# Transposing a stored matrix inside the last layer of one graph network instead of ahead of the next one

## What is computed

```python
h = jnp.maximum(_layernorm(x), 0.0); x = x + _L0_gnn_ref(h, edge_index, ...)   # sum over edges, two dense layers
h = jnp.maximum(_layernorm(x), 0.0); x = x + _L1_gnn_ref(h, edge_index, ...)   # two normed sums over edges
h = jnp.maximum(_layernorm(x), 0.0); x = x + _L2_gnn_ref(h, edge_index, ...)   # four layers, each:
#   z = segment_sum(h[src], dst) + h;  z = relu(z @ W1[i] + b1[i]) @ W2[i] + b2[i];  h = relu(batchnorm(z))
h = jnp.maximum(_layernorm(x), 0.0); x = x + _L3_gnn_ref(h, edge_index, ...)   # mixhop:
#   xj = segment_sum(val[:, None] * xj[col], row)      (the edges in the other direction)
```

## Time and profile before

| | |
|---|---|
| time, median of 3 runs | 1275.44 us (1271.63 to 1276.02) |
| the profiled execution: its own time | 1276.86 us |
| its span, first to last instruction | 1275.3 us |
| PE busy | 1142.3 us, 90% of the span |
| DVE, ACT busy | 687.3 us (54%), 456.4 us (36%) |
| mean granted clock of PE | 0.969 |

### The profile page before, as it was taken

How to read it: one execution, slowest core, us unless ns; L and a number is a source line. 1 busy time by engine, 2 the same in 40 slices (tenths; PEclk the granted TensorE clock), 3 DMA queues, 4 the chain that set the end, 5 groups by cost and what they waited for, 6 DMA issues and landing times.

```text
span 1275.3 us, 19427 instructions
## 1 busy us (share of the span) xinstructions
PE 1142.3 (90%) x6308; PEld 660.3 (52%) x6308; DVE 687.3 (54%) x2175; ACT 456.4 (36%) x1348; POOL 8.5 (1%) x31
## 2 busy tenths in 40 slices
PE   1677899998989999998998998993899998999997
PEld 1556667665554555545445445452544554444644
DVE  8999999995452235455364453466343334533211
ACT  1558988886571122211202113116211213631100
POOL 1000000000000000000000000000000000000000
PEclk9999999999999999999998998996999998999999
DMA  3100000001001000134132231338996313410001
GB/s 63 31 2 2 1 2 10 1 2 47 6 11 25 15 9 1 38 81 89 32 80 55 51 83 33 79 69 150 254 261 170 83 43 82 106 49 22 13 25 29
DMA packets 208801, 70.31 MB, mean 55 GB/s; under 512 B 180999, under 2 KB 208074, under 8 KB 208699
## 3 DMA queue, kind: packets, MB, share of 16 engines
q1 hardware_dynamic: 121131, 43.37, 14.7%
q10 hardware_dynamic: 87568, 25.67, 9.3%
HBM read 20.71 MB, written 28.26 MB: 38 GB/s over the span
## 4 chain that ended last, share of the span: by engine, by line
PE 73%; DVE 11%; ACT 4%; SPq 4%; DMA 3%; issue 3%; DVEq 1%; ACTq 0%; POOL 0%; POOLq 0%
PE PS L1156 48%; PE PS L886 7%; DVE HPb L750 4%; SPq L2077 4%; PE PS L2422 2%; PE PS L1453 2%; PE PS L875 2%; PE PS L851 2%; PE PS L1909 2%; PE PS L1915 2%; DMA ADJ<-adj_d 2%; DVE HPb L701 2%; ACT HPb L2399 1%; DMA deg_d<-ADJ 1%; PE PS L1945 1%
## 5 line engine op out<-in xcount | busy, mean ns | idle before, releaser
L1156 PE MATMUL PS<-ADJ,HPb 125*128 125x500 bf16 (+2 forms) x2450 | 492.7, 357 | 11.6 <-DMA ADJ<-adj_d 4.5
L1156 PEld LDWEIGHTS PS<-ADJ,HPb 125*128 125x128 f16 x2450 | 240.7, 99 | 258.0 <-issue 41.1
L922 ACT CAST ADJ<-PS 126x72 f32 (+7 forms) x784 | 193.4, 316 | 52.0 <-PE PS L886 18.4
L1156 PE MATMUL PS<-ADJ,Zf 125*128 125x500 bf16 (+2 forms) x1050 | 202.1, 352 | 0.0
L886 PE MATMUL PS<-HPb 128*128 128x150 bf16 (+3 forms) x784 | 191.8, 346 | 3.4 <-ACT ADJ L922 2.7
L1156 PEld LDWEIGHTS PS<-ADJ,Zf 125*128 125x128 f16 x1050 | 102.4, 97 | 93.8 <-issue 1.3
L750 DVE TENSOR_SCALAR HPb<-XRf,Zf 128x176 bf16<-128x176 f16 (+2 forms) x588 | 135.8, 291 | 1.3 <-PE PS L886 0.3
L875 PEld LDWEIGHTS PS<-HPb 128*128 128x128 bf16 x642 | 85.6, 141 | 61.7 <-issue 37.1
L1700 DVE CUSTOM_DVE_ANT_0 HPb<-ADJ,HPb 125x625 bf16<-125x625 bf16 x125 | 101.2, 810 | 3.7
L875 PE MATMUL PS<-HPb 128*128 128x25 bf16 x642 | 91.4, 214 | 13.0 <-DVE HPb L750 12.6
L1808 DVE TENSOR_SCALAR Zf<-PS,B_L 128x500 f32<-128x500 f32 (+2 forms) x28 | 19.1, 683 | 141.7 <-PE PS L1915 141.7
(11 more groups left out here) (325 smaller groups left out, 1024.3 us busy)
## 6 DMA issues: line engine op xcount, KB each, us to landing
adj_d<-ADJ ACTq DMA_DIRECT2D x25, 700.0 KB
HPb<-y_d SPq DMA_DIRECT2D x19, 187.5 KB, 2.5
HPb<-di_d SPq DMA_DIRECT2D x10, 250.0 KB, 3.5
adj_d<-ADJ ACTq DMA_DIRECT2D x25, 81.2 KB
ADJ<-in_x SPq DMA_DIRECT2D x1, 1562.5 KB
q_d<-HPb SPq DMA_DIRECT2D x25, 62.5 KB
HPb<-di_d SPq DMA_DIRECT2D x5, 305.2 KB
HPb<-s_d ACTq DMA_DIRECT2D x5, 250.0 KB, 6.7
```

The costliest lines, as they stand in the source:

```text
L922: e.copy(to, WPS[group % BANKS][0:PD, t0 * RESTS[q]:t1 * RESTS[q]] .rearrange("p (t d) -> p t d", t=t1 - t0)).then_inc(s_mv, 1)
L1156: mm = e.matmul(accs[q], H[0:PN, t, q, 0:P], cols, start=(t == 0 and (two or q == 0)), stop=(t == NT - 1 and (two or q == 1)), skip_group_ ...
```

## The change

Three things change. The stores of `keep` start one network earlier: seven of them (one a chunk) in phase `L1b`, behind ACT's copy of the sum, and six in each of the first three layers of `L2`; the last layer has none. `ADJT` is laid 240 elements (`T0`) further up, so that its first five pieces only cover columns that the chunks up to the same number have left. And `turned(0)` to `turned(4)` are issued by SP inside the last layer, each once its chunk is summed; `turned(5)` waits for the last sum, and `turned(6)` stands behind the load of the weights, ahead of the six row loads. `rows_out` now stands between `turned(3)` and `turned(4)`.

```diff
+        T0 = -(-(NT - 1) * (AW - NP) // 16) * 16
+        ADJT = ADJ[:, :, :].rearrange("p t d -> p (t d)")[:, T0:T0 + NT * NP].rearrange("p (t s) -> p t s", t=NT)
+        assert all(TURNED[c][1] + T0 <= sum(SPANS[c]) * PN for c in range(NC - 2))
...
             if act:
+                e.wait_ge(s_adj, 3)
+                e.dma_start(adj_d[N:NP], columns(0, 0, NP - N)).then_inc(s_kept, 16)
                 e.wait_ge(s_inv, 2)
...
                     e.activation(first_of(LOS, c), sums(NC + c, c)[1], ACT.Copy, scale=INVL).then_inc(E1b["lo"], 1)
+                    keep(c)
                     e.wait_ge(s_stat, n)
...
-                e.wait_ge(s_dout, 102)
-                rows_out(s1_d, DEG)
+                e.wait_ge(s_kept, 16 * (2 * NT + 1))
+                for c in range(NC - 2):
+                    if c == NC - 3:
+                        e.wait_ge(s_dout, 102)
+                        rows_out(s1_d, DEG)
+                    done(E2["agg"], (LAYERS - 1) * NC + c + 1)
+                    turned(c)
...
-                        if c < NC - 1:
-                            keep(l * (NC - 1) + c)
-                        if (l, c) == (0, 2):
-                            keep(NT - 1)
+                        if c < NC - 1 and not last:
+                            keep(NC + l * (NC - 1) + c)
...
                 e.wait_ge(s_dout, 118)
-                e.wait_ge(s_kept, 16 * (2 * NT + 1))
                 done(E2["agg"], NC * LAYERS)
-                turned(0)
-                turned(1)
+                turned(NC - 2)
                 done(E2["d2"], NC * LAYERS)
                 e.dma_start(WB[:, 0:2 * P].rearrange("p (q n) -> p q n", q=2),
                             a["L3_gnn_l1_w"][0:2].rearrange("q p n -> p q n")).then_inc(s_wt, 16)
+                turned(NC - 1)
                 e.wait_ge(s_bn["tr"], LAYERS * NB)
                 for c in range(NC - 1):
                     row_in(beside(c), di_d, c, SPANS3)
-                for c in range(2, NC):
-                    turned(c)
```

More of the change, by code:

```diff
@@ L120, in build @@
     KEPT = PN // 16 * 16
-    assert NT * NP <= NT * AW and KEPT < PN and LAYERS * (NC - 1) + 1 == NT
+    assert NT * NP <= NT * AW and KEPT < PN and NC + (LAYERS - 1) * (NC - 1) == NT
     TURNED, s0 = [], 0
@@ L275, in build @@
         IOC = XRf[:, RW:RW + HC * P // 2].bitcast(F16).rearrange("p (n c) -> p n c", c=HC)
-        ADJT = ADJ[:, :, :].rearrange("p t d -> p (t d)")[:, 0:NT * NP].rearrange("p (t s) -> p t s", t=NT)
+        T0 = -(-(NT - 1) * (AW - NP) // 16) * 16
+        ADJT = ADJ[:, :, :].rearrange("p t d -> p (t d)")[:, T0:T0 + NT * NP].rearrange("p (t s) -> p t s", t=NT)
+        assert T0 + NT * NP <= NT * AW
+        assert all(TURNED[c][1] + T0 <= sum(SPANS[c]) * PN for c in range(NC - 2))
         adj_d = dram("adj_d", [NP, NT, P], BF16)
@@ L1559, in layers, with columns, keep @@
                     sum_tiles(E1, HP, c, (acc, acc), False, 1, before)
+            def columns(t, p0, p1):
+                v = ADJ[p0:p1, t, 0:P]
+                return bass.AP(v.tensor, v.offset, [v.ap[0], [PN, NT], [1, P]])
+            def keep(t):
+                for p0, p1 in ((0, KEPT), (KEPT, PN)):
+                    e.dma_start(adj_d[t * PN + p0:t * PN + p1], columns(t, p0, p1)).then_inc(s_kept, 16)
             if dve:
@@ L1647, in row_piece, with turned @@
                     e.dma_start(ROWP[0:PN], bcast(v[r * PIECE:(r + 1) * PIECE], PN)).then_inc(s_dout, 16)
+                def turned(c):
+                    if c >= 2:
+                        e.wait_ge(s_turned[c % 2], c // 2 * 16)
+                    s0, s1 = TURNED[c]
+                    e.dma_start(ADJT[:, :, s0:s1], adj_d[s0:s1].rearrange("s t d -> s (t d)"), transpose=True)\
+                     .then_inc(s_turned[c % 2], 16)
                 done(E0["d2"], NC)
@@ L1786, in close_row_sums @@
                 e.sem_inc(s_dout, 1)
[L1788 to L1795, removed]
             def layer2(l, last):
@@ L1840, in layer2 @@
                 if act:
-                    if l == 0:
-                        e.wait_ge(s_adj, 3)
-                        e.dma_start(adj_d[N:NP], columns(0, 0, NP - N)).then_inc(s_kept, 16)
                     for c in range(NC):
```

## The result

The changed kernel takes 1280.56 us in the median of 20 runs (1278.13 to 1284.7), the kernel before 1275.85 in 20 runs beside it. The ratio is 1.0037 with a 95% interval of 1.0022 to 1.0052: 2.8 to 6.6 us slower. I had forecast 1273.0, with 1266 to 1281 as the range, so the sign is wrong, though the time lies just inside the range. The profiled execution took 1283.77 us, with a span of 1282.1.

What follows compares the result with a forecast made beforehand. PE's waits and slow stretches in L3a were taken to lose 9.9 us. A new stall of 5.5 plus a slow stretch of 1.9 less 9.9 gave -2.5 us: from a median of 1275.44 to 1273.0, range 1266.0 to 1281.0.

Steps and rivals of the forecast that it cites:

- What bounds it, and what could be gained: PE in L3a from `hidden1(0)` at 902.00 us: two waits and their slow stretches lose 9.9 us, the most to be gained.
- The first stall: PE at 907.90 us, 2.32 us behind ACT, plus 1.7 at half clock; blamed on transposes beside the load of `s1_d`.
- The stores: Stores in L1b make the last chunk's square root 0.9 us late, under 2.6 us of cover: cost 0.
- Transposes 0 to 3: SP under the last layer: 40.0 us from 809.99, ending near 850.5, all hidden with 8 us spare.
- the landing of the row loads: Six row loads behind three transposes on SP land at 907.0 us; `hidden1(0)` at 907.5 against 902.00, +5.5 us.
- "`turned(4)`: ... I take 3 us": SP's queue: 12.1 us for 496 rows plus 3 for `rows_out` ahead (bounds 0 and 7), ending 873.9.
- The rival "order within the queue": `turned(4)` data wait for the last packet of `rows_out`, up to 7 us: +1.5, 1276.9 us; chance 0.15.
- Its sign in the profile: SP's queue: `turned(4)` held 18 us or more would show the queue's order at work.
- The slow stretch: PE behind the new stall ahead of `hidden1(0)`: 1.9 us lost, as after the wait at 959.24.
- The weights: Issued by SP behind `turned(5)`, landing at 890.5 us against 890.15 wanted; costs nothing, hidden behind the input block's 2.64 us wait.

Runs made afterwards that it cites:

- tenth: Changed kernel, `rows_out` issued by ACT, `turned(4)` at once, no wait for `rows_out` landing, row loads then load of `s1_d` ahead of `turned(6)`: 1265.59 us.
- eleventh: Changed kernel with `turned(5)` and `turned(6)` behind the row loads and held until ACT's first load of `s1_d` has landed: 1265.78 us.
- first experiment: Changed kernel with the six row loads issued ahead of `turned(6)`: 1274.15 us, ratio to before 0.997.
- second experiment: Changed kernel with the six row loads issued ahead of both `turned(5)` and `turned(6)`: 1272.38 us, ratio to before 0.9962.
- 6: Changed kernel with `rows_out` issued by ACT, `turned(4)` not waiting for closed row sums, row loads ahead of `turned(6)`: 1269.86 us.
- seventh experiment: Changed kernel with `rows_out` in 125 pieces of 100 bytes instead of 3125 of 4, so its output differs: 1270.14 us.
- third: Changed kernel with `rows_out` issued by ACT in place of SP: 1276.57 us, ratio to before 0.9995.
- fifth: Changed kernel with `rows_out` issued by ACT and no SP wait for the closed row sums ahead of `turned(4)`: 1273.74 us.
- eighth: Changed kernel, `rows_out` issued by ACT, `turned(4)` at once, `turned(5)` waiting for closed row sums but not the landing of `rows_out`: 1270.28 us.
- fourth experiment: Kernel before with only the stores of `keep` moved as in the change: 1274.08 us, ratio to before 0.9977.

## Why the prediction was wrong

**What bounds it, and what could be gained: right.** I had counted 9.9 us of loss behind 902.00. Against 77.0 us in the tenth and eleventh, the kernel before has 10.8 us more, and 8.0 in its second profile. The 10.8 is 0.9 more than my bound; 0.49 us of it is a wait of PE for a transpose at 927.87 that I had left out. The first stall was indeed the transposes': the loss is 4.3 to 4.5 us in experiments 1, 2 and 6 (81.3 to 81.5 against 77.0), where a transpose runs beside the load of `s1_d`, and absent where none does. I had 2.32 + 1.7 = 4.0.

**The stores: right.** The square root of the last chunk of L1b comes 3.81 us behind the start of the copy (before 3.74) and that of the chunk before 4.27 (before 4.04), 0.3 us late in all instead of 0.9, and PE waits for neither. The forecast of 0 holds.

**Transposes 0 to 3: right.** 43.2 us where I had 40.0, over before `rows_out`; most of the excess is in `turned(0)`, held 8.9 us where the kernel before had 6.3.

**The step that failed: the landing of the row loads**, in the term "`turned(4)`: ... I take 3 us". `hidden1(0)` came 12.4 us later in the stage (45.8 against 33.4), and I had 5.5. The missing 6.9 us, term by term: the start of `turned(4)` was right (9.8 us ahead of the stage's start, forecast 9.8); held 19.3 us against 15.1, 4.2 more; `turned(5)` 13.3 against 12.5, 0.8; `turned(6)` 13.3 against 12.1, 1.2; the loads until DVE starts 916.44 - 908.10 = 8.3 against 7.9, 0.4. These are 6.6, and the rest is hand-overs. So the mechanism was right and named, and the size was off: the price of `rows_out` lay at the bound that I gave (7), and I chose 3 because I divided its busy share over all engines. The seventh experiment prices it at 7.2 us. The other 2.0 us are the rows of `turned(5)` and `turned(6)`, which I took at 24.5 ns each. The rival "order within the queue" had the right value for `rows_out` and the right sign (+1.5), and I gave it 0.15; with 2.0 more for the two transposes it would have said +3.5. Its sign in the profile, `turned(4)` held 18 us or more, is what came.

**The slow stretch** was 79.5 - 77.0 = 2.5 us against 1.9. In sum: +12.4 + 2.5 - 10.8 = +4.1 us in the profiles; the runs say +4.7. That these agree so well is luck in part: with the second profile of the kernel before, the stage differs by 125.3 - 118.3 = 7.0 us.

**Smaller misses.** The weights: I had PE waiting for them 0.4 us at most and it waited 4.33; that was hidden behind the larger stall; in the first experiment, without it, a wait of 3.80 us cost 1. Why `turned(5)` and `turned(6)` took 13.3 us here and 11.9 to 12.9 in the seventh stays open.

## What to carry to other kernels

Hiding a large transfer earlier moves it in front of whatever the same queue issues next: write down the first small load behind it, who waits for that, and when. If the large transfer has slack of its own (chunk 5 had some 50 us), hold it back by a wait until the small loads have landed: that one wait took the stage of the second experiment from 114.6 to 110.3 us and its ratio from 0.9962 to 0.9922. And for transfers of thousands of tiny pieces don't take their busy share as their price in the queue (2.7 us from the rows of before, 7.2 measured): ask when their last piece has gone.

## What the runs showed of the hardware

- 3125 elements of 4 bytes cost the transpose of 496 rows behind them in the queue 7.2 us (19.3 against 12.1), although in these 7 us their packets fill less than half of the engines' time (46.5% from 861 to 866 us, 47.9% from 866 to 868); from the other queue they cost 16.6 - 12.1 = 4.5.
- Beside a transpose, those elements took 14.3 us from issue to landing (857.96 to 872.3); beside the last store of `keep`, in the kernel before, 11.8 (858.47 to 870.26), and with nothing beside them, in the fourth experiment, 8.9.
- The granted clock stood at 0.50, the lower level of 1.2 GHz, while PE idled ahead of `hidden1(0)`. Stretches of the changed kernel (columns as in the earlier trace rows):

```profile
904.00:908.00 4.00, 1.91 (x14) 1.11 (x12) 0.00 (x0) 0.00 (x0) 0.00 (x0) 1.00 1.26 283
908.00:912.00 4.00, 0.00 (x0) 0.00 (x0) 0.00 (x0) 0.00 (x0) 0.00 (x0) 0.51 0.78 170
912.00:916.00 4.00, 0.00 (x0) 0.00 (x0) 0.00 (x0) 0.00 (x0) 0.00 (x0) 0.50 0.74 286
916.00:920.00 4.00, 3.09 (x10) 2.21 (x11) 1.31 (x3) 0.00 (x0) 0.00 (x0) 0.50 0.10 32
```

What the slow stretch behind a stall costs (the second column of the table less 77.0) hardly grows with the stall: 2.5 us behind 11.0 us, 2.7 behind 8.6 (third), 2.0 behind 6.1 (fifth), 1.8 behind 2.4 (eighth). And 2.64 us of idle time ahead of the last input block left the clock at full in the eleventh, where 3.96 us in the fourth did not.
